# Sixteen-headed cross-attention: the next exponential moved between the two copies of a unit's transposed probabilities

## The reference, cut to what matters

```
qh = _split_heads(q @ Wq + bq)          # 16 heads of 8 features
kh = _split_heads(k @ Wk + bk)
vh = _split_heads(v @ Wv + bv)
att = jnp.einsum('bhqd,bhkd->bhqk', qh, kh) * scale
att = jax.nn.softmax(att, axis=-1)
out = jnp.einsum('bhqk,bhkd->bhqd', att, vh)
out = out.transpose(0, 2, 1, 3).reshape(b, n, h * dh)
return out @ Wo + bo
```

## Time and profile before

| | |
|---|---|
| median of three executions | 1726.67 us (1726.04 to 1728.31) |
| the profiled execution | 1730.95 us |
| its span, first to last instruction | 1729.2 us |
| TensorE, VectorE, ScalarE busy | 1219.0, 1162.2, 780.6 us |
| mean granted clock of TensorE | 0.825 |

### The profile page before, as it was taken

How to read it: one execution, slowest core, us unless ns; L and a number is a source line. 1 busy time by engine, 2 the same in 40 slices (tenths; PEclk the granted TensorE clock), 3 DMA queues, 4 the chain that set the end, 5 groups by cost and what they waited for, 6 DMA issues and landing times.

```text
span 1729.2 us, 24437 instructions
## 1 busy us (share of the span) xinstructions
PE 1219.0 (70%) x8742; PEld 779.5 (45%) x8754; DVE 1162.2 (67%) x2766; ACT 780.6 (45%) x1466; POOL 225.8 (13%) x170
## 2 busy tenths in 40 slices
PE   4998888974489999799933698987988920000685
PEld 2655555542357777545522354554654410000453
DVE  2655557877667887577767577686775449997354
ACT  1544355764355555346545432665342313442342
POOL 2210101300012233211111000310000000000121
PEclk7888798996789999889967676999999965555698
DMA  3000300000000000000000000000000320001100
GB/s 120 13 13 9 125 27 10 7 1 0 1 1 1 1 1 7 7 7 7 7 1 0 1 1 7 7 8 1 1 0 20 81 57 0 0 0 37 31 13 19
DMA packets 28856, 28.15 MB, mean 16 GB/s; under 512 B 12240, under 2 KB 23504, under 8 KB 27856
## 3 DMA queue, kind: packets, MB, share of 16 engines
q1 hardware_dynamic: 28752, 26.76, 5.3%
HBM read 20.20 MB, written 6.55 MB: 15 GB/s over the span
## 4 chain that ended last, share of the span: by engine, by line
PE 48%; DVE 23%; issue 14%; ACT 9%; POOL 2%; DVEq 2%; DMA 1%; SPq 1%; POOLq 0%; ACTq 0%
PE PSA L898 3%; PE PSA L888 3%; PE PSA L1323 2%; PE PSA L738 2%; DVE BIG L2622 2%; PE PSA L744 2%; PE PSA L721 2%; PE PSA L1005 2%; PE PSA L1017 2%; ACT BIG L1593 2%; PE PSA L1052 2%; DVE BIG L2614 2%; ACT QK L1600 2%; PE PSA L1061 2%; PE PSA L1296 2%
## 5 line engine op out<-in xcount | busy, mean ns | idle before, releaser
L1600 ACT ACTIVATE QK<-PSA 128x512 f32<-128x512 f32 x192 | 104.8, 595 | 110.5 <-PE PSA L898 110.3
L1353 PE MATMUL PSA<-ROWS,ONES 1*128 1x512 f32 x8 | 5.4, 760 | 205.0 <-DVE BIG L2661 205.0
L559 POOL TENSOR_TENSOR RSTD<-VEPS,HALF 128x4 f32<-128x4 f32 x41 | 41.7, 1017 | 649.0 <-DVE VEPS L1951 649.0
L2070 DVE TENSOR_TENSOR BIG<-PSA,MX 128x1024 f32<-128x1024 f32 x96 | 117.6, 1225 | 12.3 <-PE PSA L898 9.4
L888 PE MATMUL PSA<-BIG 32*128 32x512 f32 x384 | 114.6, 687 | 14.8 <-DVE BIG L2070 13.7
L2066 DVE TENSOR_REDUCE MX<-PSA 128x8 f32<-128x1024 f32 x96 | 116.8, 1217 | 6.2 <-PE PSA L888 5.6
L565 POOL TENSOR_SCALAR BIG<-BIG,COLS 128x512 f32<-128x512 f32 x52 | 80.6, 1569 | 260.7 <-ACT BIG L1585 140.3
L1593 ACT ACTIVATE BIG<-BIG 128x1024 f32<-128x1024 f32 x96 | 101.8, 1060 | 25.2 <-DVE BIG L2070 25.2
L898 PE MATMUL PSA<-K,BIG 128*128 128x128 f32 x768 | 107.1, 285 | 6.4 <-ACT BIG L1593 4.8
L898 PEld LDWEIGHTS PSA<-K,BIG 128*128 128x128 f32 x768 | 91.0, 147 | 40.5 <-ACT BIG L1593 28.5
L1353 PEld LDWEIGHTS PSA<-ROWS,ONES 1*128 1x128 f32 x8 | 1.4, 214 | 207.2 <-issue 207.1
(11 more groups left out here) (394 smaller groups left out, 3085.6 us busy)
## 6 DMA issues: line engine op xcount, KB each, us to landing
CTX<-in_ctx_t SPq DMA_DIRECT2D x16, 256.0 KB, 3.2
W<-in_w SPq DMA_DIRECT2D x1, 2048.0 KB, 7.5
W<-in_w SPq DMA_DIRECT2D x1, 1412.0 KB, 11.9
ROWS<-in_rows SPq DMA_DIRECT2D x1, 1232.0 KB, 9.2
scratch_q<-TMP SPq DMA_DIRECT2D x4, 256.0 KB, 2.0
W<-scratch_q SPq DMA_DIRECT2D x64, 16.0 KB
W<-in_w SPq DMA_DIRECT2D x2, 512.0 KB, 10.9
scratch_q<-BIG SPq DMA_DIRECT2D x4, 256.0 KB, 2.3
```

Of the source, the lines that this page charges most:

```text
L1600: act.activation(PT[:, m % 2, c, :], PS[4 + c], ACT.Copy).then_inc(p_ready.sem, 1)
L2070: dve.tensor_tensor(tile(PH[:, m % 2, :], 8), s, last(high, P), ALU.subtract).then_inc(shifted.sem, 1)
```

## The change

On ScalarE, in the three cross-attentions, the two copies of a unit are called one by one, and the next unit's exponential is called between them. In even units the copy of bank 6 (`values_out`) keeps its place behind the second copy, and so comes behind the exponential. The waits of each step are as before. Nothing else is changed.

```
-                def copies(m):
-                    if m >= 2:
+                def copy(m, c):
+                    if m >= 2 and c == 0:
                         act.wait_ge(pv_done.sem, pv_done.at(p, 0, m - 2))
-                    for c in range(2):
-                        act.wait_ge(t_psum.sem, t_psum.at(p, 0, 2 * m + c))
-                        act.activation(PT[:, m % 2, c, :], PS[4 + c], ACT.Copy).then_inc(p_ready.sem, 1)
+                    act.wait_ge(t_psum.sem, t_psum.at(p, 0, 2 * m + c))
+                    act.activation(PT[:, m % 2, c, :], PS[4 + c], ACT.Copy).then_inc(p_ready.sem, 1)
...
-                    copies(m)
+                    copy(m, 0)
+                    if m + 1 < GROUPS * HALVES:
+                        exp(m + 1)
+                    copy(m, 1)
                     if m and m % 2 == 0:
                         values_out(m // 2 - 1)
-                    if m + 1 < GROUPS * HALVES:
-                        exp(m + 1)
```

## The result

The changed kernel takes 1751.24 us (median of three executions, 1750.36 to 1758.22) against 1726.67 (1726.04 to 1728.31): 1.0148 times the time before, 95% interval 1.0127 to 1.0168. It is slower, as forecast, but by about twice the 11.6 us of the forecast and outside its range. The profiled execution took 1751.24 us, with a span of 1749.5.

A forecast was written before the change was run, and what follows sets the result against it. No engine is full; the order of waits bounds the kernel. Terms 2.5 + 2.0 + 1.9 + 1.3 + 2.3 + 2.0 - 0.4 = 11.6 us on 1726.67 give 1738.3 us, range 1731 to 1746.

The forecast's parts named there:

- the one on the clock: In the three stages: new stalls of up to 1.2 us leave TensorE's granted clock at 1.00, adding nothing.
- the rival that the clock falls: Half clock in one L2x-like unit in each of twelve groups: up to 42 us, about 1780 us, chance 0.03.
- (a): L0x three times, L2x's first group twice: turn waits for the value copy alone, 0.5 us later each, 2.5 us.
- (b): Exponential waits for VectorE's subtraction and drags the copies along: 2.0 us in L0x, 1.9 in L2x, 1.3 in L1x.
- (c): Last pairs of L1x and L2x: value copy behind a waiting exponential delays turn and transposes, 2.3 us together.
- (d): Six more places (L0x group seams and last group, first groups of L1x and L2x): 0.2 to 0.6 each, 2.0 us taken.
- Hidden anyway: VectorE sets the pace in the groups' second half and the turn mostly awaits other things: 1726.7 us, chance 0.07.
- smaller: VectorE swallows turn delays at L1x and L2x seams and much of L0x's: 1732 to 1735 us, chance 0.11.
- Larger: L1x and L2x pairs after the value projection also late (+3.0), eight more turns moved (+7.7): 1741 to 1749 us, chance 0.10.
- Faster: Transposes' 37 waits for the exponential shrink and no turn is late: at most 17.8 us gained, 1708.9 us, chance 0.05.

The follow-up runs named there:

- mended filled version: Changed kernel with idle transposes in TensorE's waits in seven units, L2x's only ahead of the turn: 1742.14 us, 1.0068 of the kernel before.
- two-unit run: Kernel before, with the new ScalarE order in units 10 and 18 of L0x alone: 1.0032 of the kernel before, L0x 130.20 us.

## Why the prediction was wrong

**The step that failed is the one on the clock**: "by the row they add none. I take none", with 0.03 for the rival that the clock falls. The row was read rightly and stands after the change too (1201 to 1212 us: 6.64 of 11 us busy, clock 1.00), but it did not say what waits in the middle of the other units' work would do. New waits of TensorE of 1.0 to 2.3 us (at the end of L1x 2.29 us, where it was 0.82) brought falls of 3.4 us. What a fall costs follows from how much later than before the last turn of a stage comes, counted from the first exponential. In L0x that is 6.89 us in the changed kernel and 5.30 in its mended filled version, so 1.6 for one fall. In L1x it is 4.20 and 2.57, of which 0.25 is a clock that rose half a microsecond sooner, so 1.4. In L2x it is 7.44 and 2.09, of which 1.8 is a clock that rose 4.4 us sooner, so 3.5 for three falls; the run with four idle transposes gives the same 3.5. The five falls took 6.5 us, then, and 1.0 us more is half clock behind the last turns of L1x and L2x, where the stages end 4.58 and 8.08 us later than before: 7.5 us of clock, which the sum put at nothing. In the two-unit run 4.54 us stand against 10.2 us at half clock.

The Trainium skill, "TensorE: Matmul & The Clock Gate", section "Part 1: The HAM clock gate", lets idleness halve the array's clock and activity give it back. The rows agree with that much: the falls stand behind waits, and the clock is full again 3.4 us later. The row that I set against it, of L2x's last units, was of another stretch. The rival's price was wrong as well: 42 us for twelve units, 3.5 each, where a fall costs 1.2 to 1.6 and five came.

**The order of the waits was right; that its sum came out so closely is in part luck.** With the falls filled, the last turn of each stage comes later than before by 5.30 us in L0x, 2.8 in L1x and 3.9 in L2x (the latter two with the 0.25 and 1.8 us of a sooner clock put back); forecast were about 5, 2.7 and 4. The sum, 12.0, stands against 11.6, and the medians of that run differ by 11.8. By steps, from the starts of line 898 in the mended run and in the kernel before:

- (a) 0.55 us each, in L0x (four times, not three) and in L2x's first group (twice); forecast 0.5.
- (b) 1.07 us in L0x and 1.07 at each of L2x's two seams, 0.67 at L1x's; forecast 1.0, 0.95, 0.64.
- (c) 1.13 us in L1x, 1.12 in L2x; forecast 1.15.
- (d) The seams of L0x take 0.45 each, its last group 1.27, over the bound of 0.96, L1x's first group 0.2 twice, and L2x's 0.6: 3.7 us, forecast 2.0.

Steps (a), (b) and (d) thus came to 2.9 us more than forecast. Give-backs of up to 0.5 us at single units of L0x and L2x, 2.9 us in all where the forecast had 0.4, make up for it.

**The rivals.** "Hidden anyway" and "smaller" fall: VectorE swallows hardly any of the places. "Larger" names the right side for the wrong reason. "Faster" fails as stated, since the turn is ahead of the transposes; in the pair of runs with the turn behind the product the sign turns round.

**The 24.6 us between the medians** are then 19.55 in the stages (12.0 of order and 7.5 of clock), 0.7 outside them, and the 4.28 by which one profile of the kernel before lay over its median; its executions in later comparisons ran from 1722.1 to 1737.6 us. So the clock is 7.5 of the 12.9 us that the forecast missed. Another 4.3 is a term that no run bears out: the forecast took 4.28 us off, from 1742.6, because the profile of before lay over its median, and the changed kernel's profiled execution is itself the median. Beside those later executions the changed kernel lost 15.4 us when it ran again, with three falls in its profile.

Left open is why one wait brings a fall and another does not: the same waits of 0.7 and 1.0 us did at one unit and not at the like one eight units later, and in the runs with the value copy late alone and with four idle transposes waits of 0.72 us and 0.54 or 0.44 us were enough at the first of these units. Chance of an execution is not all of it. L2x had the same three falls, 65, 106 and 130 us after its first exponential, in the changed kernel and in the run with one unit of L0x kept busy, where its clock rose 13.8 us after that exponential; when the changed kernel ran again the clock rose after 9.6 us, and of the three one was left, at 126 us.

## What to carry to other kernels

Before moving an instruction forward on an in-order engine, list what it passes and who waits for that; the sign came from the one copy that a TensorE instruction ahead of the released work needs, and where that copy is not passed (the odd units) the same move gains. Order such a run by when inputs are ready, for an instruction that waits drags along all behind it. And count new waits of about 1 us on TensorE twice: once by the delay, and once as a chance of 1.2 to 1.6 us lost to half clock, for here the clock took two fifths of what the stages lost.

## What was not expected of the hardware

Behind a wait of 1.03 us, with one of 0.71 us two microseconds before it, TensorE ran at half clock for 6.8 us, in a stage where it had been at full clock for over 30 us; 13 idle transposes in such waits kept the clock up there without costing time.

The work ahead of L0x, which no kernel here changes, took 261.1 to 261.9 us up to the first exponential in some of the profiled executions and 266.1 to 267.5 in the others. Two windows of it, first in the profile of the kernel before, then in that of the changed kernel:

```profile
65.00:130.00 65.00, 58.60 (x484) 37.09 (x486) 36.82 (x61) 31.46 (x52) 16.09 (x11) 0.87 0.07 17
130.00:195.00 65.00, 55.33 (x472) 33.92 (x472) 35.33 (x59) 29.90 (x50) 7.45 (x6) 0.86 0.04 9
```

```profile
65.00:130.00 65.00, 58.79 (x468) 37.08 (x465) 34.61 (x51) 29.86 (x50) 14.57 (x10) 0.82 0.07 17
130.00:195.00 65.00, 56.60 (x456) 36.33 (x452) 36.15 (x66) 30.39 (x49) 8.96 (x7) 0.82 0.04 9
```

The longer one has the lower granted clock; what decides between the two was not tried. Differences under 5 us between single profiles of this kernel are best read by stage.
